# Thirteenth sequence's first reads of Q and K ordered behind the read back of the twelfth's attention rows

## The reference

```python
# x: (4, 512, 288); c: (4, 288); blocks 0 to 3
mod = silu(c) @ w_ada + b_ada
sh1, sc1, g1, sh2, sc2, g2 = split(mod, 6)
h = layernorm(x) * (1 + sc1) + sh1
q, k, v = split(h @ w_qkv + b_qkv)          # 16 heads x 18
# blocks 0, 1, 3: softmax over the 512 rows, head by head
# block 2: scores = einsum('nthd,ntkd->nthk'): softmax over the 16 heads of one row
o = softmax(q k^T / sqrt(18)) v
x = x + g1 * (o @ w_proj + b_proj)
h = layernorm(x) * (1 + sc2) + sh2
# blocks 1 to 3: one feed-forward of 1152 hidden values
# block 0: four experts, the best two of each row mixed by gate weights
x = x + g2 * (gelu(h @ w1 + b1) @ w2 + b2)
```

## Time and profile before

| | us |
|---|---|
| median of 3 runs | 2202.05 |
| lowest, highest | 2201.2, 2202.48 |
| profiled execution, its own time | 2202.24 |
| span of the profile, first to last instruction | 2200.5 |
| PE busy | 2004.8 |
| DVE busy | 1336.7 |
| ACT busy | 1142.4 |

### The profile page before, as it was taken

The page is one execution under the profiler, slowest core; times in us unless marked ns, Lnnn a source line. Parts: engine busy times, 40 slices in busy tenths (PEclk is TensorE's granted clock), DMA queues, the critical chain, the costliest instruction groups (busy, mean ns, idle before and its releaser), DMA issues.

```text
span 2200.5 us, 38987 instructions
## 1 busy us (share of the span) xinstructions
PE 2004.8 (91%) x15592; PEld 1496.7 (68%) x15592; DVE 1336.7 (61%) x2940; ACT 1142.4 (52%) x1705; POOL 208.3 (9%) x311
## 2 busy tenths in 40 slices
PE   6988999899998999999899999989997898999998
PEld 4346578748974896698575566887886646474658
DVE  4747647656674677476658482463545858684842
ACT  2353734474656365545636556554344474747463
POOL 3000111111110110011110000001100000000001
PEclk9686999899989999999999999998899999999999
DMA  5234242343234232524331412446154141314101
GB/s 160 60 120 85 74 122 63 73 122 92 77 68 136 64 86 48 152 67 100 78 104 18 131 7 65 68 78 134 30 107 111 31 114 36 96 20 112 26 3 25
DMA packets 204731, 173.97 MB, mean 79 GB/s; under 512 B 54822, under 2 KB 164678, under 8 KB 204550
## 3 DMA queue, kind: packets, MB, share of 16 engines
q1 hardware_dynamic: 197974, 158.76, 31.0%
q0 software_dynamic: 6576, 12.71, 2.1%
HBM read 125.57 MB, written 40.11 MB: 75 GB/s over the span
## 4 chain that ended last, share of the span: by engine, by line
PE 61%; DVE 20%; ACT 11%; DMA 3%; issue 3%; SPq 2%; POOL 0%; ACTq 0%; POOLq 0%; DVEq 0%
PE PSA L1890 16%; PE PSA L1905 14%; DVE MX L1529 9%; PE PSA L1680 5%; PE PSA L1794 4%; PE PSA L1771 4%; PE PSA L1741 4%; ACT PB L1378 4%; PE PSA L1784 3%; PE PSA L1753 2%; DVE HH L1659 1%; PE PSA L1814 1%; PE PSA L1703 1%; DVE FL L1429 1%; ACT FH L1408 1%
## 5 line engine op out<-in xcount | busy, mean ns | idle before, releaser
L1529 DVE TENSOR_REDUCE MX<-PSA 128x1 f32<-128x512 f32 x768 | 490.2, 682 | 292.9 <-PE PSA L1771 289.8
L1890 PE MATMUL PSA<-A,FH 128*128 128x256 f32 x2520 | 442.1, 290 | 14.0 <-DVE HH L1659 9.9
L1905 PE MATMUL PSA<-FH,HH 128*128 128x288 f32 x2016 | 443.2, 311 | 3.9 <-DVE HH L1659 3.3
L1415 ACT ACTIVATE HH<-PSA 128x512 fp32r<-128x512 f32 x252 | 150.6, 598 | 561.5 <-PE PSA L1890 552.0
L1378 ACT ACTIVATE PB<-PSA 128x1024 f32<-128x1024 f32 x384 | 370.8, 1026 | 86.4 <-PE PSA L1784 85.8
L1890 PEld LDWEIGHTS PSA<-A,FH 128*128 128x128 f32 x2520 | 362.3, 194 | 37.4 <-issue 18.7
L1905 PEld LDWEIGHTS PSA<-FH,HH 128*128 128x128 f32 x2016 | 327.1, 193 | 41.0 <-issue 32.6
L1905 PE MATMUL PSA<-FL,HH 128*128 128x288 f32 x1008 | 301.7, 299 | 0.0
L1771 PE MATMUL PSA<-KS,QS 54*128 54x512 f32 x768 | 221.4, 504 | 29.8 <-DVE MX L1529 12.2
L1283 POOL TENSOR_TENSOR X<-X,TM 128x288 f32<-128x288 f32 x128 | 101.3, 809 | 1455.2 <-DVE TM L1594 1455.2
L1659 DVE TENSOR_TENSOR HH<-PSA,HH 128x512 fp32r<-128x512 f32 x252 | 172.1, 683 | 85.1 <-ACT PSA L1416 84.5
(11 more groups left out here) (171 smaller groups left out, 2258.8 us busy)
## 6 DMA issues: line engine op xcount, KB each, us to landing
qkd<-HH SPq DMA_DIRECT2D x48, 504.0 KB
ST<-in_L_cond_w SPq DMA_DIRECT2D x51, 432.0 KB
ST<-in_L_cond_w SPq DMA_DIRECT2D x102, 192.0 KB
QS<-qkd SPq DMA_DIRECT2D x88, 144.0 KB
KS<-qkd SPq DMA_DIRECT2D x88, 144.0 KB
QS<-qkd SPq DMA_DIRECT2D x144, 72.0 KB
KS<-qkd SPq DMA_DIRECT2D x144, 72.0 KB
ST<-in_L_cond_w SPq DMA_DIRECT2D x153, 48.0 KB
```

The costliest lines, as they stand in the source:

```text
L1415: e.activation(r(HH[u][:, 0, :]), PS[bk][:, :], gelu)
L1529: e.reduce_max(MX[p // 2 % 2][:, col:col + 1], PS[bk][:, :], axis=AX.X).then_inc(free[bk], 1)
L1890: m = e.matmul(PS[bk][:, s_ * 256:(s_ + 1) * 256], r(w_), r(x_[:, half * 256:(half + 1) * 256]), start=(z == 0), stop=(z == 6))
L1905: m = e.matmul(PS[bk][:, 0:C], r(HH[u][:, c, tk]), r(w_), start=False, stop=(j == NCH - 1 and z == 2))
```

## The change

In `proj_qk` for item 12, the reads of groups 0 and 1 are no longer put after the second and the fourth tile. `at_end`, which so far named item 0 alone, names item 12 too, and both groups are put at the end, once the step that reads `OT` back for item 11 is in the list (`n_otr` counts these steps; the fourth is item 11's). Group 2 follows behind as before. The time stamps `qk_at` that the planner takes with the reads come later as well, and with them the score pairs of item 12.

```diff
-    at_end = (0,)
+    at_end = (0, 12)
@@ proj_qk
             if t == 3 and i not in at_end:
                 while s2_at[0] < (i - 1, 1):
                     yield
                 qk_in(i, 2, 4, 1, outs[3])
         if i == 12:
+            while n_otr[0] < 4:
+                yield
+            qk_in(i, 0, 2, 0, outs[1])
+            qk_in(i, 2, 4, 1, outs[3])
             return
```

## The result

| | before | changed |
|---|---|---|
| median, us | 2202.05 (11 runs) | 2209.51 (11 runs) |
| lowest, highest | 2196.77, 2203.16 | 2202.49, 2213.92 |
| profiled execution, its own time | 2202.24 | 2204.01 |

The ratio is 1.0038, with a 95% interval of 1.002 to 1.0055: slower by 7.5 us, where 7.5 was forecast.

What follows compares the result with a forecast made beforehand. TensorE, busy for 91% of the span, was taken to bound the kernel. On 2202.24 us, -7.5 + 2.0 + 10.5 + 2.5 = +7.5 gave 2209.7, or 2209.5 for the median; range 2204.5 to 2213.5.

Steps and rivals of the forecast that it cites:

- `scr` leaves at 1680.6 when its data is there: On SP after item 11's attention: `scr` would leave at 1680.6 instead of 1694.19, and `OT` land at 1690.8 instead of 1704.4.
- First score pair waits 0.9: On PE at item 12's first score pair: arriving at 1695.0, it waits 0.9 for group 0's reads, landing at 1695.9.
- The starving pairs: Rival at item 12's first score pairs: group 0's reads land at 1699.1, everything after 3.2 later, 2212.7 in all; chance 0.12.
- The 3.0 of slow clock go: On PE behind the wait for `OT`: the half clock over 6.6 us would vanish, saving 3.0 us.
- +1.0 for VectorE: Before item 12's s2 step 0: two more pairs of maxima on VectorE would cost 1.0 us.
- ScalarE: At item 12's first exps: they follow the last turn of XN by 6.34 us, so they start at 1746.9.
- the first gain: At the start of item 12's attention: 7.5 us gained, not 9.6.
- Step 12: In item 12's attention: PE waits 10.5 us, from 1789.3 to 1799.8, for group 3's maxima to be transferred into QS.
- Four pairs at 0.5 each and the clock at 2.5: In item 12's attention: four score pairs moved in add 2.0 us for PE; half clock behind step 12's wait adds 2.5.
- The rest hides: Remaining moved work: costs nothing, as no instruction is added or removed and the displaced loads are used much later.
- this rival (0.09): In the feed-forward after item 12's attention: its 7.0 us without PE work give the stall back, 2202.5; chance 0.09.
- Step 8: Rival in item 12's attention: group 2's maxima transfers come late behind the weight load, +2 us, 2211.5; chance 0.07.

Runs made afterwards that it cites:

- E4: Kernel before with only item 12's group 1 reads put behind the read of `OT`, group 0's reads left in place: 2187.33 us, ratio 0.9966.
- E2: Kernel before with only PE's order changed: item 12's time stamps come late, both groups' reads stay where they were: 2213.12 us, ratio 1.0085.
- E3: Changed kernel with two score pairs instead of one behind each of steps 0 to 5 of item 12's attention: 2204.53 us, ratio 1.0027.
- E5: Changed kernel with item 13's group 1 reads held until item 12's last maxima are in the list: 2207.42 us, ratio 1.0037.
- E8: The kernel before, unchanged, run again for a second profile: 2191.65 us, one run.
- E6: The changed kernel, unchanged, run again on another chip: 2209.36 us, ratio 1.0048.
- E1: Kernel before with only SP's order changed: both groups' reads moved, time stamps taken where they were: 2202.05 us, ratio 1.0035.

## Why the prediction was right, step by step

**`scr` leaves at 1680.6 when its data is there: wrong.** Its data were there in time, but from V12 it left at 4.1, not 1.2. I had put nothing for SP's issuing of the last HH writes, and SP stood at two of them for 1.62 and 5.14 us. `scr` itself landed as foreseen, in 4.58 (for 4.74); group 0's last read landed 4.54 behind the start of its issue, at 1688.86. The lateness of 2.9 at `scr` is 2.8 at the issue of `OT` and 2.0 at the first score pair.

**First score pair waits 0.9: mis-sized, 3.34.** Of the 2.4 more, 2.0 is that lateness, and 0.5 that PE was there earlier than computed (15.1 from V12, foreseen 15.6). The starving pairs, a rival with 0.12, came in part (2.0 of its 3.2), and through SP's issue, not through slow reads.

**The 3.0 of slow clock go: the step that failed.** I took the half clock to belong to the wait for `OT`. It moved with PE's wait, to behind the new one of 3.34. Three windows show it, each from the first turn of `OT` or the first pair to the last turn of XN: the kernel before, E4, and the changed kernel.

```profile
1704.47:1748.08 43.61, 40.08 (x233) 31.04 (x234) 34.99 (x78) 12.78 (x22) 1.57 (x2) 0.93 0.20 39
1689.91:1731.39 41.48, 37.31 (x234) 28.94 (x233) 35.48 (x79) 12.77 (x22) 1.57 (x2) 1.00 0.28 62
1688.90:1734.80 45.90, 42.78 (x249) 33.40 (x250) 37.19 (x81) 11.99 (x22) 1.80 (x2) 0.93 0.18 55
```

With the clock at 1.00 throughout, E4 has 2.8 us less PE work for the same instructions, but the stretch is only 2.1 shorter; waits for DVE take back the rest. The changed kernel has 0.93, as before. From the first pair to the last turn of XN I had 44.7 us (1740.6 - 1695.9), and it was 45.9, 1.2 more: that the 3.0 stayed costs 2 to 3, and the +1.0 for VectorE didn't come, since PE's waits in this stretch are 2.96 us, against 3.42 before. This split is argued; the total of 1.2 is measured. The Trainium skill, "TensorE: Matmul & The Clock Gate", section Terms, has half where the rows have 46%; an estimate by it is 3.05 us for the 6.1 us at half clock, where the 46% gives 2.8, and the measurement can't tell the two apart.

**ScalarE: right.** The exps came 6.33 behind the last turn of XN, where I had 6.34. Step 0 came 3.7 behind this turn and not 1.5, since PE waited 0.60 and 1.48 for rows of DVE, but that cost the exps nothing. So the first gain was 4.3 us: 7.5, less 2.0, less 1.2.

**Step 12: right in place and size.** Foreseen 10.5 us of waiting; 8.42 and 2.06 make 10.5. The mechanism is shown: E2 has it without any moved read of item 12, E3 removes it by earlier pairs, E5 takes 3.9 us off the wait by the queue's order. What I had not seen is its split: part of it stands ahead of the maxima's turn, on DVE. PE itself came to this turn at 113.7 from V12 (1786.16 - 2.06 - 1670.45); 109.9 was foreseen (1789.3 - 1679.42) for step 12. The lateness of the first place, 3.2, makes most of the difference, and SP's chain stood as much later: step 12 at 124.4, 120.4 foreseen.

**Four pairs at 0.5 each and the clock at 2.5: their sum is right but for 0.7.** From the first exps to item 13's values the kernel before takes 52.0, the changed one 66.4: 14.3, against 10.5 + 2.0 + 2.5 = 15.0. The clock's part is smaller, with 3.15 us of PE work at half clock, worth at most 1.6. The pairs' part is larger than 2.0 by then: DVE's maxima of the moved pairs stand ahead of the subtractions for the tiles, and PE waits 0.98 for HH L1527 several times instead of once.

**The rest hides: right within the spread.** From item 13's values to the end 394.7 us against 394.1. Nothing is given back in the next feed-forward; this rival (0.09) fell. Step 8 didn't wait.

**Sum.** By the first pair of profiles -4.3 + 14.3 + 0.7 = +10.7, and with E8 as the base +7.5; the timings give +7.5, and in E6 ratio 1.0048, 10.6. The cost is thus 7 to 11 by these figures (4.4 to 12.1 by the interval of the first timing), and the forecast of 7.5 sits at its lower edge. The first gain was 3.2 too large and the loss at the second place 0.7 too large, which should have put the measurement 2.5 above the forecast; that the medians met it is chance. The sign "the end at 2208" did not come in the profile (2202.2), because that execution was 9.0 us ahead at V12.

## What to carry to other kernels

A read that blocks a more urgent transfer is best moved only as far as its consumer allows: here half of the move (group 1) wins 0.3 to 0.5%, and the whole of it loses 0.4%. In a planned program, look at what a moved step drags along: the time stamps moved the score pairs, and these alone (E2) cost 10.7 to 12.3 us up to item 13's values, where the whole change cost 7.8 to 10.0. Removing a wait of TensorE also returns the slow clock behind it, but only if no other wait of a few us takes its place.

## What the hardware showed that I had not expected

- Issuing a DMA is not always short on SP. The 72 writes of HH in the kernel before have a median of 0.34 us and a longest of 1.76. In the changed kernel one took 5.14, with other HH writes and nothing but these and a GB row ahead of it; in E1 it took 5.14 too, in E6 5.57. In E4 the last three took 1.34, 6.52 and 0.58. The long one was each time one of the last tile's two, which are the smallest (36x2x512). What it waited for the profile doesn't say, and no run here tests it.
- A wait of 3.34 us is followed by more than 6 us at half clock, as a wait of 7.44 is; behind one of 8.42 it was between 3 and 4. The length of the slow stretch behind a wait didn't follow the length of the wait here.
- Two executions of the same kernel came to V12 13.9 us apart (1679.42 and 1665.52), while the 521 to 524 us behind it agreed within 3.2. Comparing spans of single profiles would have given +1.7 us for the change. The windows ahead of V12, of the first profile and of E8, have the same instructions, with 12.4 us less PE work and a higher granted clock in the second:

```profile
0.00:1679.40 1679.40, 1536.39 (x12547) 1176.13 (x12548) 1015.70 (x2267) 863.59 (x1307) 187.48 (x283) 0.94 0.36 86
0.00:1665.50 1665.50, 1523.96 (x12547) 1170.25 (x12548) 1015.46 (x2267) 863.82 (x1307) 187.13 (x283) 0.95 0.36 87
```
